# Softmax row maxima of an attention: one of eight products per period replaced by a product with a key difference, taken by relu and a sum-and-maximum

## The reference

```
q = rope(h @ Wq.T); k = rope(h @ Wk.T); v = h @ Wv.T       # layer 0; no rope in the second one
scores = einsum("blhd,bshd->bhls", q, k) / sqrt(16)
weights = softmax(scores, axis=-1)                          # over 2048 keys
out = einsum("bhls,bshd->blhd", weights, v)
```

## Time and profile before

| | |
|---|---|
| median of 3 runs | 3439.08 us (3438.27 to 3440.1) |
| profiled execution, its span | 3437.2 us; the median of the runs is 1.9 us above it |
| busy | PE 3289.5 us (96%), DVE 2955.9 (86%), ACT 2473.5 (72%), POOL 580.5 (17%) |
| exps of the attentions, L957 | 4096, 2142.0 us busy |
| takes of the maxima, L981 | 2928, 2292.0 us of busy time as merged by the page |

### The profile page before, as it was taken

The page is one execution under the profiler, slowest core; times in us unless marked ns, Lnnn a source line. Parts: engine busy times, 40 slices in busy tenths (PEclk is TensorE's granted clock), DMA queues, the critical chain, the costliest instruction groups (busy, mean ns, idle before and its releaser), DMA issues. The chain is left out here.

```text
span 3437.2 us, 66173 instructions
## 1 busy us (share of the span) xinstructions
PE 3289.5 (96%) x25137; PEld 1521.3 (44%) x25138; DVE 2955.9 (86%) x4695; ACT 2473.5 (72%) x4700; POOL 580.5 (17%) x601
## 2 busy tenths in 40 slices
PE   8999999999999999888899889999999999999997
PEld 5433333333333333567677656533333333333332
DVE  8889999999999997353787665499999999999991
ACT  4178888888888888533333324688888888888886
POOL 4410000000000000053331143133333210000001
PEclk9689999999999999889999999999999999999999
DMA  8451220202021100345010376513132231202001
GB/s 270 138 140 47 41 39 15 44 16 39 15 44 32 24 15 5 129 135 191 27 36 12 121 248 200 139 35 58 35 52 45 52 64 27 44 16 40 15 16 49
DMA packets 306934, 232.77 MB, mean 68 GB/s; under 512 B 205591, under 2 KB 257720, under 8 KB 301970
## 3 DMA queue, kind: packets, MB, share of 16 engines
q1 hardware_dynamic: 290308, 179.45, 22.6%
q0 software_dynamic: 14832, 47.79, 4.3%
q10 hardware_dynamic: 1504, 1.64, 0.1%
HBM read 126.49 MB, written 102.76 MB: 67 GB/s over the span
## 5 line engine op out<-in xcount | busy, mean ns | idle before, releaser
L957 ACT ACTIVATE att_l_probs<-att_l_s_ps 128x512 f32<-128x512 f32 x4096 | 2142.0, 599 | 309.5 <-PE att_l_s_ps L900 269.3
L981 DVE TENSOR_REDUCE att_in_part_max<-att_l_max_ps 128x1 f32<-128x512 f32 (+1 forms) x2928 | 2292.0, 885 | 9.9 <-PE att_l_max_ps L890 9.5
L915 PE MATMUL att_l_o_ps<-att_l_probs,att_l_v_sb 128*17 128x512 f32 (+2 forms) x11776 | 1171.5, 470 | 1.4 <-DMA att_l_v_sb<-v_rows 1.1
L900 PE MATMUL att_l_s_ps<-att_in_q_sb,att_in_k_sb 50*128 50x512 f32 x2048 | 734.4, 453 | 10.1 <-DVE att_l_o_ps L995 9.0
L900 PE MATMUL att_l_s_ps<-att_in_q_sb,att_l_k_sb 50*128 50x512 f32 x2048 | 727.0, 453 | 1.3
L890 PE MATMUL att_l_max_ps<-att_l_k_sb,att_in_q_sb 50*128 50x512 f32 x2048 | 722.4, 445 | 5.2 <-DVE att_in_part_max L981 5.2
L890 PE MATMUL att_l_max_ps<-att_in_k_sb,att_in_q_sb 50*128 50x512 f32 x1856 | 660.0, 449 | 5.0 <-DVE att_in_part_max L981 4.8
L890 PEld LDWEIGHTS att_l_max_ps<-att_l_k_sb,att_in_q_sb 50*128 50x128 f32 x2048 | 336.2, 184 | 319.7 <-DVE att_in_part_max L981 297.8
L900 PEld LDWEIGHTS att_l_s_ps<-att_in_q_sb,att_l_k_sb 50*128 50x128 f32 x2048 | 328.6, 184 | 267.5 <-ACT att_l_probs L957 238.4
L900 PEld LDWEIGHTS att_l_s_ps<-att_in_q_sb,att_in_k_sb 50*128 50x128 f32 x2048 | 335.1, 186 | 241.3 <-ACT att_l_probs L957 202.3
L890 PEld LDWEIGHTS att_l_max_ps<-att_in_k_sb,att_in_q_sb 50*128 50x128 f32 x1856 | 307.8, 186 | 290.5 <-DVE att_in_part_max L981 268.4
(11 more groups left out here) (264 smaller groups left out, 2758.3 us busy)
## 6 DMA issues: line engine op xcount, KB each, us to landing
att_in_q_sb<-q_hi SPq DMA_DIRECT2D x256, 64.0 KB
slot_rows<-att_l_zeros POOLq DMA_DIRECT2D x10, 1024.0 KB, 4.5
ffn_parts<-slot_rows SPq DMA_DIRECT2D x40, 256.0 KB, 3.1
tile_out<-ffn_parts SPq DMA_DIRECT2D x40, 256.0 KB, 2.2
att_in_q_sb<-q_lo SPq DMA_DIRECT2D x128, 72.0 KB
att_l_v_sb<-v_rows SPq DMA_DIRECT2D x16, 544.0 KB, 15.2
att_in_k_sb<-k_hi SPq DMA_DIRECT2D x32, 256.0 KB, 8.9
att_l_k_sb<-k_hi SPq DMA_DIRECT2D x32, 256.0 KB, 9.4
```

Source lines behind the costliest of these rows:

```text
L900: nc.tensor.matmul(s_ps[:, c % SB], k_sb[j // GPB % 2][rows, pair, u * P:(u + 1) * P], q_sb[rows, j % QR, pair], start=True, stop=True).th ...
L915: last = nc.tensor.matmul(o_ps[32 * h:32 * h + AUG, c0:c1], v_sb[:, j // GPB % 2, u, h * AUG:(h + 1) * AUG], probs[:, (n * KT + u) % PB, h ...
L957: nc.scalar.activation(probs[:, (n * KT + u) % PB, h], s_ps[:, c % SB], ACT.Exp, scale=float(HD) ** -0.5).then_inc(exp_done, 1)
L981: nc.vector.reduce_max(dst, banks, AX.X).then_inc(units_taken, 1)
```

## The change

For one head of each pair (`RISE_HALF` = 0) the maxima of the key parts 2 and 3 are no longer two units. With the keys k2 and k3 of the two parts, max(q.k2, q.k3) = q.k2 + relu(q.(k3 - k2)). So the product of part 3 becomes a product with the difference of the keys, the *rise*. It goes to a bank of the score ring, ScalarE takes its relu into `above`, and VectorE adds it to the unit of part 2 (the *base*) and takes the maximum in one instruction. The place of the part that isn't used in `part_max` is set once to a very small number.

In a period: unit 5 is the rise (`RISE_AT`), unit 7 the base (`BASE_AT`). ScalarE has nine activations; the relu is between the exps of c4 and c5, and the score ring counts it (`exp_act`, `acts_before`). The seven other units go round the 4 banks in order (`HELD`), and VectorE takes them in four instructions. The difference of the keys, in high and low parts, is made by GpSimd in both stages ahead, stored by SP, and loaded with the keys of each head group (3 more transfers; `NK` is the count waited for).

```diff
-NQ, NK, NSH = 16 * 6, 16 * 6, 16 * 2 * NSHIFT
+NQ, NK, NSH = 16 * 6, 16 * 9, 16 * 2 * NSHIFT
...
+RISE_AT, BASE_AT = 5, 7
+PART_OF = (0, 0, 1, 1, 2, 3, 3, 2)
+HELD = tuple(i for i in range(UNITS) if i != RISE_AT)
 MB = 4
-TAKES = ((0,), (1, 2), (3,), (4,), (5, 6), (7,))
+TAKES = ((0, 1), (2, 3), (4, 5), (6,))
...
+        def acts_before(p):
+            return UNITS * p + min(p, PERIODS)
+        def rise_act(p):
+            return acts_before(p) + RISE_AT
+        def exp_act(n, u, h):
+            w, c = u // STEP_TILES, u % STEP_TILES * HG + h
+            p = period_of(n, w)
+            return acts_before(p) + c + (p < PERIODS and c >= RISE_AT)
...
     # TensorE, maximum(n, w, i)
-                behind, held = divmod(UNITS * p + i - MB, UNITS)
-                if behind >= 0:
-                    pe.wait_ge(units_taken, behind * len(TAKES) + TAKE_OF[held] + 1)
+                if i == RISE_AT:
+                    c = rise_act(p)
+                    pe.wait_ge(exp_done, c - SB + 1)
+                    nc.tensor.matmul(s_ps[:, c % SB], q_sb[rows, j % QR, pair, tile * P:(tile + 1) * P],
+                                     rise_sb[j // GPB % 2][rows, pair], start=True, stop=True).then_inc(s_ready, 1)
+                    return
+                held = HELD.index(i)
+                if held >= MB:
+                    pe.wait_ge(units_taken, p * len(TAKES) + TAKE_OF[held - MB] + 1)
+                elif p > 0:
+                    before = max(x for x in range(len(HELD)) if x % MB == held)
+                    pe.wait_ge(units_taken, (p - 1) * len(TAKES) + TAKE_OF[before] + 1)
...
     # TensorE, scores; ScalarE, exps: the same for both
-                c = n * EXPS + u * HG + h
+                c = exp_act(n, u, h)
...
+            def take_rise(p):
+                if p >= PERIODS:
+                    return
+                c = rise_act(p)
+                act.wait_ge(s_ready, c + 1)
+                if p > 1:
+                    act.wait_ge(units_taken, (p - 1) * len(TAKES))
+                nc.scalar.activation(above[:, p % 2], s_ps[:, c % SB], ACT.Relu).then_inc(exp_done, 1)
...
+                        if u % STEP_TILES * HG + h == RISE_AT:
+                            take_rise(period_of(n, u // STEP_TILES))
                         exps(n, u, h)
...
     # VectorE, take_units
+                if HELD[units[0]] == BASE_AT:
+                    dve.wait_ge(exp_done, rise_act(p) + 1)
+                    nc.vector.tensor_tensor_reduce(above[:, p % 2], max_ps[:, units[0] % MB], above[:, p % 2], 1.0, BELOW,
+                                                   ALU.add, ALU.max, part_max[:, g % 2, first:first + 1]).then_inc(units_taken, 1)
+                    return
...
     # GpSimd in project_layer0, for each pair i of token groups
+                for a in range(2):
+                    nc.gpsimd.tensor_tensor(rise[:, a], whole[:, 1, 2 + a], whole[:, 0, 2 + a], ALU.subtract).then_inc(rise_ready, 1)
...
+                for a in range(2):
+                    nc.gpsimd.tensor_copy(rise_parts[:, a, 0], rise[:, a]).then_inc(rise_hi_ready, 1)
+                pool.wait_ge(rise_hi_ready, i * 2 + 2)
+                for a in range(2):
+                    nc.gpsimd.tensor_tensor(rise_parts[:, a, 1], rise[:, a], rise_parts[:, a, 0].bitcast(F32), ALU.subtract).then_inc(rise_lo_ready, 1)
...
     # the stage ahead of the second attention: GpSimd ahead of a batch's scatters, SP ahead of its next loads
+                take_rise(b)
                 pool.wait_ge(put_ready, b + 1)
...
+                if q == GPB - 1:
+                    store_rise(b)
```

More of the change, by code:

```diff
@@ L256, in first_maxima @@
             rows = slice(half * HROWS, half * HROWS + XROWS)
-            last = nc.tensor.matmul(ps[:, k % 2 * 2 + half], ai.q[rows, j, pair, tile * P:(tile + 1) * P],
+            last = nc.tensor.matmul(ps[:, k % 2 * 2 + 1 - half], ai.q[rows, j, pair, tile * P:(tile + 1) * P],
                                     ai.k[0][rows, pair, part * G:(part + 1) * G], start=True, stop=True)
@@ L438, in _ @@
             pool.wait_ge(ln.z_ready, TPG)
-            set_shift_rows(nc, ai.k[0], ai)
-            pool.wait_ge(ai.rows_set, 2)
-            with pool.Fori(0, PAIRS_OF) as i:
+            set_shift_rows(nc, ai.k[0], ai.rise[0], ai)
+            pool.wait_ge(ai.rows_set, 3)
+            for i in range(PAIRS_OF):
                 for slot in range(2):
@@ L656, in softmax_attention @@
         q_sb, k_sb = ai.q, [ai.k[0], sb("k_sb1", [P, PAIRS, T], F32R)]
+        rise_sb = [ai.rise[0], sb("rise_sb1", [HROWS, PAIRS, G], F32R)]
+        above = sb("above", [P, 2, G])
         v_sb = sb("v_sb", [P, 2, TPB, VROW])
@@ L686, in softmax_attention @@
         assert NIT == B
-        EXPS = KT * HG
         STEPS = NIT * NB
@@ L975, in take_units @@
                     return
-                g, k, half = unit_of(n, w, units[0])
-                first = 2 * k + half
-                dst = part_max[:, g % 2, first:first + 1] if len(units) == 1 else part_max[:, g % 2, first:first + 4:3]
+                g, k, half = unit_of(n, w, HELD[units[0]])
+                first = 2 * k + 1 - half
+                dve.wait_ge(unit_ready, len(HELD) * p + units[-1] + 1)
+                if HELD[units[0]] == BASE_AT:
[3 more added lines that the diff above has]
+                    return
+                _, k1, half1 = unit_of(n, w, HELD[units[-1]])
+                apart = 2 * k1 + 1 - half1 - first
+                dst = part_max[:, g % 2, first:first + 1 + apart:max(apart, 1)]
                 banks = max_ps[:, units[0] % MB:units[0] % MB + len(units)]
-                dve.wait_ge(unit_ready, UNITS * p + units[-1] + 1)
                 nc.vector.reduce_max(dst, banks, AX.X).then_inc(units_taken, 1)
@@ L2009, in store_parts, with store_rise @@
                         sync.dma_start(dst, parts[:, n % 2, a, part].bitcast(F32)).then_inc(stored[n % 2], 16)
+            def store_rise(b):
+                for a in range(2):
+                    sync.wait_ge(rise_lo_ready, b * 2 + a + 1)
+                    for part, dram in enumerate((io.rise_hi, io.rise_lo)):
+                        dst = dram[ds(b, 1)].rearrange("a h c t -> (a h) c t")[a * NHH:(a + 1) * NHH, :, T // 2 - G:T // 2]
+                        sync.dma_start(dst, rise_parts[a][:, part].bitcast(F32)).then_inc(rise_stored, 16)
             for n in range(N):
@@ L2049, in _, with take_rise @@
             sync.wait_ge(v_stored, N * 16)
+            sync.wait_ge(rise_stored, B * 16 * 4)
         @block.gpsimd
         def _(pool):
+            def take_rise(b):
+                n = b * GPB + GPB - 1
+                first, second = parts[:, 0].bitcast(F32), parts[:, 1].bitcast(F32)
+                for a in range(2):
+                    done = b * 2 + a
+                    pool.wait_ge(lo_ready, n * 4 + 2 + a + 1)
+                    if done > 0:
+                        pool.wait_ge(rise_lo_ready, done)
+                    for part in range(NPART):
+                        nc.gpsimd.tensor_tensor(rise[:, part], second[:, 2 + a, part], first[:, 2 + a, part], ALU.subtract).then_inc(parts_read, 1)
+                    pool.wait_ge(parts_read, done * 2 + 2)
+                    nc.gpsimd.tensor_tensor(rise[:, 0], rise[:, 0], rise[:, 1], ALU.add).then_inc(rise_step, 1)
+                    pool.wait_ge(rise_step, done + 1)
+                    if b > 0:
+                        pool.wait_ge(rise_stored, b * 16 * 4)
+                    nc.gpsimd.tensor_copy(rise_parts[a][:, 0], rise[:, 0]).then_inc(rise_hi_ready, 1)
+                    pool.wait_ge(rise_hi_ready, done + 1)
+                    nc.gpsimd.tensor_tensor(rise_parts[a][:, 1], rise[:, 0], rise_parts[a][:, 0].bitcast(F32), ALU.subtract).then_inc(rise_lo_ready, 1)
             nc.gpsimd.memset(va[:].rearrange("p t (h c) -> p (t h) c", c=AUG)[:, :, HD:AUG], 1.0).then_inc(ones_set, 1)
```

89 lines of the change are left out of this document (65 added, 24 removed).

## The result

The changed kernel takes 3842.43 us (median of 4 runs, 3838.93 to 3845.23), the kernel before 3439.59 (4 runs, 3438.27 to 3442.9): a ratio of 1.117, 95% interval 1.115 to 1.119. It is 403 us slower. The profiled execution took 3838.93 us, its span is 3837.1.

The account below looks back on a forecast made before the run. VectorE's reductions were taken as the bound, TensorE hardly behind. The span of 3437.2 us plus 442 for the attentions and 5 for the stages ahead gave 3884, 3886 as median of the runs; range 3735 to 3945.

Parts of the forecast that it names:

- the loop that was forecast: Attention: TensorE and ScalarE wait for each other through late product 4, relu and score c7; 5.70 us a period.
- The bound: Mid attention: VectorE's reductions set the pace at 4.65 us a period, TensorE's own order needs 4.69.
- Rival B: Attention: faster, the loads decide and not the loop; TensorE's order of 4.69 remains, 3412 us; chance 0.07.
- Score c7 waits for the relu: Score ring: c7 waits for the relu, not exp c4, moving everything behind it in TensorE's queue; 5.38 us a period.
- Product 4 is late: Attention: product 4 waits for the first take of two banks; 224-column values start 2.56 after c0, not 2.24.
- Rival A: Attention: product 4 isn't late, bank 0 comes free sooner; 5.38 a period, 3749 us; chance 0.14.
- The sum-and-maximum: VectorE's new operation: a slot of 0.60 us, bounds 0.53 and 1.13; VectorE then 3.99 a period against 4.65.
- Rival C: VectorE: slow sum-and-maximum of x sets the period at x + 4.19 above x = 1.5; about 4230 us; chance 0.04.
- Rival D: ScalarE: each relu reloads tables, 1.28 before and after; 6.97 busy a period, about 4520 us; chance 0.02.
- Relu by ScalarE: Attention: a ninth activation of 0.49 makes ScalarE 4.41 busy; relu by VectorE instead estimated at 4.59 a period.
- The stages: Stages ahead of the attentions: 5 us taken, from 0 to 9; the first 0, up to 2.
- Signs: Mid attention: VectorE busy about 70%, ScalarE below 85%, step 45 us, 224-column values 2.5 us after c0.

Follow-up runs that it names:

- The kernel with both rings and the rise beside c3: Against the changed kernel: four score banks, three banks for the maxima in an unbroken round, single takes, rise product beside c3; 3454.73 us (1.0048).
- The pair with eight and nine activations: Changed kernel without rise product and relu, sum-and-maximum adding zeros: 3581.6 us; with a ninth activation, a relu of a constant tile taking no score bank: 3584.08 us.
- the first experiment: Changed kernel with five takes in place of four, unit 0 taken alone; 3723.86 us (1.082).
- the experiment with four and three banks: Against the changed kernel: four score banks, three for the maxima, begun anew each period, all seven units taken alone; 3603.09 us (1.047).

## Why the prediction was right

The forecast was 3886 us with a range of 3735 to 3945, slower at 0.91. It came out at 3842, by the loop that was forecast. That the error is no greater than 44 us is partly luck: the attentions were put 64 us too high and the stages ahead 17 too low. By its steps:

| step | forecast | measured |
|---|---|---|
| c0 to c1 | 0.34 | 0.34 |
| c1's product to the first take | 0.50 | 0.43 |
| the take | 1.24 | 1.22 |
| signal to product 4 | 0.06 | 0.05 |
| to the 224 columns | 0.42 | 0.43 |
| to c5 | 0.50 | 0.50 |
| to the relu | 0.59 | 0.54 |
| relu to c7 | 0.65 | 0.65 |
| to the 512 columns | 0.42 | 0.42 |
| to c0 | 0.98 | 0.98 |
| period | 5.70 | 5.57 (the steps as rounded add up to 5.56) |
| first period of a step | 5.49 | 5.47 |
| step | 45.4 | 44.44 |
| stages ahead | 5 | 22 |

- **The bound.** Right. VectorE was the bound with TensorE's order just behind. The kernel with both rings and the rise beside c3 shows it from the other side: there VectorE has 16 us of 300 to spare, and the seven later periods fall by 0.04 only. Rival B's 3412 was too low all the same: it had 4.80 for a step's first period, taken from periods without maxima, where the kernel before had 5.21 with them.
- **Score c7 waits for the relu.** Right, in 486 of 488 periods. The pair with eight and nine activations shows that it isn't the work, which is 0; the rise product, its bank and the waits through them are 258 us.
- **Product 4 is late.** Right, 0.30 a period forecast as 0.32. Rival A said 3749 for its absence, the first experiment has 3724.
- **The terms.** The attentions cost 378 us and not 442. Two latencies were taken from rows that are a little longer than what happens here: product to take, 0.50 for 0.43, and score to relu, 0.59 for 0.54. They are 0.12 of the 0.13 of the period, and with 7 x 61 periods 51 of the 64 us. The stages took 17 of these back.
- **The sum-and-maximum.** 0.60 as a slot was right (0.606 from its start to the read, which is 0.08 long). Rival C needed 1.5. But its circle was nearer than I had it: x + 4.19 gives 4.79 at 0.60, more than TensorE's 4.69. With the relu's bank out of the way the period is 4.94, and what stands second is of this kind: in the kernel without the relu products wait 550 times for a take and 253 times for the sum-and-maximum. It isn't quite the circle that I added up, since VectorE waits for products too. I had costed it as a rival for slow operations only.
- **Tables.** There are 18 table loads before and 18 after, none of them between the first and the last exp of an attention. Rival D is out, as the Trainium skill had it (page "ScalarE: Activation LUTs", section "Table sets: the hidden batching unit": relu is in every set); the trace agrees.
- **Relu by ScalarE.** The Trainium skill, same page, section "Rules for kernel authors", sends it to VectorE. Here ScalarE's time for it cost nothing (3581.6 us without a ninth activation, 3584.08 with one); what cost was where it stands in the ring. Relu by VectorE was not tried.
- **The stages.** This step failed: 22 and not 5. I had hidden GpSimd's new work in its gaps and took VectorE's operations beside it to be as long as alone. In the first stage, put at 0 to 2, it is 8.8: VectorE's four normalizing operations took 3.63 us beside the subtractions where they had taken 1.38, and all 32 went from 13.5 to 20.9 us busy. In the stage between the attentions, 13.0, the wait that I had priced at 5 hardly grew: TensorE waits 3.96 us for the expert rows, not 3.23. Four normalizing operations took 4.25 us there beside GpSimd and not 1.38, and with four small operations that also run beside it VectorE's are about 6 us longer; its longest wait for the store of the value rows, which SP issues in order, went from 8.4 to 11.7. These are 10 of the 13; the rest is open.
- **Signs.** VectorE's share fell to 79%, not 70 (3.99 of 5.70 had left out its small operations, and that a take which waits for its product lasts 1.22 and not the slot of 1.13); ScalarE's to 84%, as said; the 224 columns start 2.48 after c0, as said.

The loss of a later period, 5.57 - 4.71 = 0.86, parts so by the runs: 0.63 (5.57 to 4.94) goes when the rise product and the relu's bank go, and 0.23 is left with the four takes and the sum-and-maximum, which hold banks that products want. The late product 4 is in both, 0.30 while the relu is there. None of this is more work, as the kernel with both rings and the rise beside c3 shows. What no run shows is whether rings of four and three would help the kernel before. And no version here is faster than the kernel before: what the change saves is VectorE's time, and TensorE's order needs about 4.7 us with or without it.

## What to carry to other kernels

Before moving work off the busiest engine, add up the order of the next one; here it was 0.04 us a period behind, and that is all that the best version got back in seven periods of eight. An operation that reads from a ring of buffers takes a slot in it, and its cost is the wait of whatever comes a ring's length later, not its own time: ask which slot, behind which product, and who is queued behind the waiter. Taking two buffers in one instruction saves the engine time and holds both until the end; when the producer is in order, that can cost more than it saves, and a wait removed is worth only the distance to the next one.

## What the runs showed of the hardware that I had not expected

VectorE and GpSimd hold each other up on operands in SBUF. In the kernel before, VectorE's four normalizing operations, beside a GpSimd subtraction that ended at 42.38, 0.2 us after they began, and didn't lengthen them:

```profile
42.17 1.38 DVE L137 TENSOR_SCALAR qkv_ln_z<-all_x_res,qkv_ln_mv,qkv_ln_rstd 128x256 f32 x4
```

With the change the single ones are 0.41, 1.35, 1.35 and 0.75 us: the second begins at 42.14 and the third at 43.41, just after each of GpSimd's subtractions (41.98 and 43.30), and each ends 0.15 us after that one. They take turns by whole instructions, as far as these rows show. The Trainium skill says this: page "SBUF — State Buffer", section "Who interferes with whom", that only the port pair shared by the two engines contends, that it is an exclusive lock, and that whoever issues first has it for the whole instruction. The trace agrees (1.35 us for an operation of 0.41). By the same section of the Trainium skill a VectorE instruction with two inputs in SBUF contends with a GpSimd instruction that reads it. The 1.10 us of L533 beside the casts agree.

A take frees its bank later than it frees VectorE: short takes follow each other at 0.60 us, but the product that waits for one comes 0.05 behind its full 0.68; behind the sum-and-maximum it comes 0.74 after the start (0.61 to the read, 0.08 for it, 0.05). With three banks such differences show: in the experiment with four and three banks the 0.74 is a term of its 4.96.
